# A LayerNorm input of a local-attention network: one half of its shifted copy moved from ScalarE to VectorE

## What is computed

```
def shift_tokens(t):
    a, s = jnp.split(t, 2, -1)
    s = jnp.pad(s, ((0, 0), (1, 0), (0, 0)))[:, :-1]
    return jnp.concatenate([a, s], -1)

def ffn_layer(x, g, bln, W1, b1, W2, b2):
    mu = x.mean(-1, keepdims=True)
    var = ((x - mu) ** 2).mean(-1, keepdims=True)
    xn = (x - mu) / jnp.sqrt(var + 1e-05) * g + bln
    hg = xn @ W1 + b1
    a, gate = jnp.split(hg, 2, -1)
    return a * jax.nn.gelu(gate, approximate=False) @ W2 + b2

for i in range(DEPTH):
    x = attn_layer(shift_tokens(x), Wqkv[i], q_scale[i], k_scale[i], Wo[i]) + x
    x = ffn_layer(shift_tokens(x), ln_g[i], ln_b[i], W1[i], b1[i], W2[i], b2[i]) + x
```

## Time and profile before

| | us |
|---|---|
| median of 3 runs | 1779.91 |
| lowest and highest run | 1777.05 to 1782.78 |
| the profiled execution | 1762.38 |
| its span | 1760.6 |
| TensorE busy | 1601.1 |
| DVE busy | 1228.2 |
| ACT busy | 1153.2 |
| POOL busy | 1003.2 |

### The profile page before, as it was taken

How to read it: one execution, slowest core, us unless ns; L and a number is a source line. 1 busy time by engine, 2 the same in 40 slices (tenths; PEclk the granted TensorE clock), 3 DMA queues, 4 the chain that set the end, 5 groups by cost and what they waited for, 6 DMA issues and landing times. The chain is left out here.

```text
span 1760.6 us, 75862 instructions
## 1 busy us (share of the span) xinstructions
PE 1601.1 (91%) x33590; PEld 1298.7 (74%) x33590; DVE 1228.2 (70%) x1912; ACT 1153.2 (65%) x2115; POOL 1003.2 (57%) x757
## 2 busy tenths in 40 slices
PE   5879999989999999999999899999999999999976
PEld 4557778777777877877777777777778777777765
DVE  7666677677677667767767776776776777677662
ACT  2246676767767766776776666776676676767644
POOL 2155566666565756646666664675565586566551
PEclk9999999999999999999999999999999999999996
DMA  3266665675765567566567656657755666665650
GB/s 129 57 169 148 154 144 135 152 182 134 165 151 127 137 153 198 132 147 157 122 153 201 144 130 145 154 126 186 169 135 138 153 146 143 150 157 123 151 125 25
DMA packets 98568, 252.97 MB, mean 144 GB/s; under 512 B 30016, under 2 KB 36288, under 8 KB 97472
## 3 DMA queue, kind: packets, MB, share of 16 engines
q1 hardware_dynamic: 98240, 248.12, 59.0%
HBM read 44.59 MB, written 2.10 MB: 27 GB/s over the span
## 5 line engine op out<-in xcount | busy, mean ns | idle before, releaser
L805 DVE SCALAR_TENSOR_TENSOR UV<-ps,veca,rope 128x512 f32<-128x512 f32 x768 | 531.2, 744 | 184.5 <-PE ps L381 155.3
L1212 POOL TENSOR_TENSOR KK<-UV 128x512 f32<-128x512 f32 x192 | 241.9, 1282 | 406.6 <-DVE UV L805 403.4
L957 ACT ACTIVATE sq<-ps 128x512 f32<-128x512 f32 (+1 forms) x400 | 228.1, 583 | 263.0 <-PE ps L381 172.4
L1212 POOL TENSOR_TENSOR Qtb<-UV 128x512 f32<-128x512 f32 x192 | 242.9, 1287 | 86.5 <-DVE UV L805 86.5
L381 PE MATMUL ps<-xh,wh 128*128 128x256 f32 x768 | 245.1, 319 | 1.7 <-ACT sq L957 0.8
L1231 POOL TENSOR_TENSOR E<-E,ri 128x1024 f32<-128x1024 f32 x96 | 182.8, 1904 | 79.3 <-DVE ri L878 73.6
L381 PEld LDWEIGHTS ps<-PT,V 64*64 64x64 f32 x12288 | 194.1, 136 | 40.0 <-issue 35.4
L381 PE MATMUL ps<-xh,wl 128*128 128x256 f32 x768 | 218.0, 284 | 3.8 <-issue 3.8
L381 PE MATMUL ps<-xl,wh 128*128 128x256 f32 x768 | 217.7, 283 | 1.0 <-issue 1.0
L381 PE MATMUL ps<-PT,V 64*64 64x32 f32 x12288 | 210.3, 221 | 3.6 <-ACT PT L957 2.0
L1222 POOL TENSOR_TENSOR E<-E,mx 128x1024 f32<-128x1024 f32 x96 | 182.9, 1905 | 51.3 <-DVE mx L872 51.2
(11 more groups left out here) (128 smaller groups left out, 3106.0 us busy)
## 6 DMA issues: line engine op xcount, KB each, us to landing
V<-Vs SPq DMA_DIRECT2D x672, 128.0 KB
KK<-KK SPq DMA_DIRECT2D x384, 128.0 KB
Qtb<-Qtb SPq DMA_DIRECT2D x384, 128.0 KB, 2.4
rope<-in_c_rope SPq DMA_DIRECT2D x48, 512.0 KB, 4.1
raw<-in_Wqkv SPq DMA_DIRECT2D x6, 1536.0 KB, 7.9
V<-Vs SPq DMA_DIRECT2D x96, 64.0 KB
V<-V SPq DMA_DIRECT2D x96, 64.0 KB, 2.0
wo<-in_Wo SPq DMA_DIRECT2D x6, 512.0 KB, 6.5
```

Of the source, the lines that this page charges most:

```text
L805: e.scalar_tensor_tensor(UV[:, p % 2, slot, :].rearrange("p (i t) -> p i t", i=2), ps[:, half, :].rearrange("p (i t) -> p i t", i=2), veca ...
L957: return e.activation(out, in_, f, **kw)
L1212: e.tensor_tensor(dst, u, v, op).then_inc(s["rot_done"], 1)
```

## The change

On DVE a new entry `c_xz` stands right behind `c_xb`. It waits until DVE's own residual has been written and until `zl` of the step before has been computed, and copies rows 0 to 63 of the residual to `zs`. ACT's `c_xs` keeps the copy of rows 64 to 127. It waits for DVE's copy, by the new semaphore `zx_done`, in place of `zl_done`. `z_act` is then raised once a step, and `c_mu` waits for that. The list gains one entry; its line breaks are new, the order of the others isn't.

```diff
-    b_sub0 b_s0 a_rot1 b_nrm0 a_sqx0 a_mx1 b_s1 a_my1 a_x1 a_y1 c_xb a_sqy1 a_rl c_wo w_h0 b_s2 b_sum0 b_sub1
+    b_sub0 b_s0 a_rot1 b_nrm0 a_sqx0 a_mx1 b_s1 a_my1 a_x1 a_y1 c_xb c_xz a_sqy1 a_rl c_wo w_h0 b_s2 b_sum0 b_sub1
...
             def c_mu(j, _):
-                e.wait_ge(s["z_act"], j * 2 + 2)
+                e.wait_ge(s["z_act"], j + 1)
                 mm(ps[:, WO, 0:T], cen[:, :], zs[:, :]).then_inc(s["mu_done"], 1)
...
+            def c_xz(j, _):
+                x0 = j % 2 * T
+                e.wait_ge(s["xb_done"], j * C + C)
+                if j:
+                    e.wait_ge(s["zl_done"], j)
+                e.tensor_copy(zs[0:hf, :], XB[0:hf, x0 + 1:x0 + 1 + T]).then_inc(s["zx_done"], 1)
...
                 e.wait_ge(s["xb_done"], j * C + C)
                 e.wait_ge(s["cb_done"], j // 2 + 1)
-                if j:
-                    e.wait_ge(s["zl_done"], j)
-                act(zs[0:hf, :], XB[0:hf, x0 + 1:x0 + 1 + T]).then_inc(s["z_act"], 1)
+                e.wait_ge(s["zx_done"], j + 1)
                 act(zs[hf:, :], XB[hf:, x0:x0 + T]).then_inc(s["z_act"], 1)
```

More of the change, by code:

```diff
@@ L57 @@
 SCHEDULE = """b_rcq a_mx0 a_xs+1 a_vs0 a_v0 a_v1 b_rq a_my0 a_x0 a_xh+1 b_scale0 a_rot0 a_vs1 a_y0 b_lnq b_max0 a_sqy0 b_rqt
-    b_sub0 b_s0 a_rot1 b_nrm0 a_sqx0 a_mx1 b_s1 a_my1 a_x1 a_y1 c_xb a_sqy1 a_rl c_wo w_h0 b_s2 b_sum0 b_sub1
+    b_sub0 b_s0 a_rot1 b_nrm0 a_sqx0 a_mx1 b_s1 a_my1 a_x1 a_y1 c_xb c_xz a_sqy1 a_rl c_wo w_h0 b_s2 b_sum0 b_sub1
     a_norm0 a_xl+1 w_h1 a_sqx1 b_exp0 c_xs c_zl a_rck c_mu w_l0 b_s3 c_var b_nrm1 c_zsq a_halo a_x2 a_lnk a_rot2
[L60 to L63, removed]
+    c_rs a_rot3 a_y2 a_rh a_sqy2 b_pt0 b_pto0 b_scale1 b_pt1 c_zh b_att0 w_l2 b_max1 b_att1 a_sp0 b_pto1 a_sqx2 c_h0
+    c_zn b_exp1 a_mx2 a_sp1 a_my2 b_oto0 c_gelu0 b_sum1 b_wo a_x3 c_wl c_gelu1 a_kn0 b_pto2 c_h1 b_pt2 c_hm0 a_y3
+    a_kn1 a_mx3 a_sqy3 a_sqx3 b_pt3 c_hm1 c_wh b_att2 c_h2 a_norm1 w_h2 a_my3 c_hm2 b_att3 b_pto3 c_down c_gelu2
+    c_fin b_xb w_l1 b_oto1""".split()
 LAG = {"w": 0, "a": 0, "b": 1, "c": 2}
@@ L237, in program @@
             rh_done rl_done rkb_done khat_done k_halo rqt_done rq_done s_done e_done m_done sub_done p_done rs_done
-            ri_done pt_done pts_done pn_done o_done ots_done wo_done xb_done cb_done z_act mu_done
+            ri_done pt_done pts_done pn_done o_done ots_done wo_done xb_done cb_done z_act zx_done mu_done
             zsq_done var_done zln_done rstd_done zn_done zb_done zh_done zl_done h_done gelu_done hm_done w2_done
@@ L950, in _ @@
             run({"a_mx": a_mx, "a_my": a_my, "a_rck": a_rck, "b_rcq": b_rcq, "a_kn": a_kn, "b_rq": b_rq, "b_scale": b_scale,
-                 "b_max": b_max, "b_sum": b_sum, "b_xb": b_xb, "c_xb": c_xb, "c_zn": c_zn,
+                 "b_max": b_max, "b_sum": b_sum, "b_xb": b_xb, "c_xb": c_xb, "c_xz": c_xz, "c_zn": c_zn,
                  "c_hm": c_hm, "c_fin": c_fin}, tail)
```

## The result

| | before | after |
|---|---|---|
| median, us | 1771.55 | 1777.76 |
| lowest and highest | 1754.40 to 1782.78 | 1771.05 to 1788.24 |
| runs | 20 | 20 |
| the profiled execution | 1762.38 | 1772.32 |
| its span | 1760.6 | 1770.5 |

The ratio is 1.0045, with a 95% interval of 1.0025 to 1.0065: +8.0 us (4.4 to 11.5). The runs of before have a lower median here than the three shown ahead of the prediction (1779.91), so the absolute times of the prediction lie some 8 us high; what it says of the change is not touched by that.

The account below looks back on a forecast made before the run. TensorE, busy 91% of the span, bounds the kernel, its wait for zs lying on the path. 37 steps x 0.11 us = +4.1 us, the other 11 nothing; 1779.91 + 4.1 = 1784.0 us, range 1769 to 1790.

Parts of the forecast that it names:

- TensorE's hole for zs sets the step: At the product of zs with cen, TensorE waits 28.2 us in 37 steps; any loss or gain there passes on whole.
- nothing behind zs runs by a clock of its own: Later TensorE holes (PT, the queries' DMA) end with work TensorE itself released, so they move along with zs.
- The copy alone, 0.28 us: DVE's 64x256 copy to zs takes 0.28 us without POOL, reckoned from SBUF-to-SBUF copies of 512 and one column.
- The copy is held by POOL: DVE's copy behind XB waits for POOL's running rotation half to end at 867.41, and itself ends at 867.56.
- ScalarE's half starts at 867.59: ACT's copy starts 0.03 us behind DVE's, ends at 868.00; the matmul starts at 868.05, 0.11 us later than before.
- the likeliest one (0.50): DVE's copy is held until POOL's instruction ends: +0.11 us in each of 37 steps, +4.1 us; chance 0.50.
- a copy that isn't held (-9.2 us): Rival: DVE's copy to zs runs freely beside POOL; each of 37 steps gains 0.25 us, 1770.7 us; chance 0.18.
- one at a single rate (-4): Rival: DVE's copy moves one column at a time, unheld, 0.42 us; -0.11 us a step, 1776 us; chance 0.05.
- The slow release (+8.9 us): Rival: DVE's held copy ends 0.28 us behind POOL's end, not 0.15; +0.24 us a step, 1788.8 us; chance 0.17.
- POOL's second half in front (+49 us): Rival: POOL's second rotation half goes before DVE's copy, which waits to 868.63; +1.33 us a step, 1829 us; chance 0.05.
- Removed ACT copies bring nothing further, `rs` is 0.31 us late and covered at the transposes: Dropping 48 ScalarE copies (20 us busy) gains nothing more; DVE's sum over E, 0.31 us late, delays no transposes.
- the two covers (0.56 and 0.50 us): Slack behind DVE's copy: 0.56 us before TensorE wants POOL's normalised E, 0.50 us before DVE's E<-ps; both absorb 0.31 us.

Follow-up runs that it names:

- side by side: Changed kernel, but ScalarE's half no longer waits for DVE's copy and the product with cen waits for both halves; 0.9965 of the kernel before, median 1764.32 us.
- the second experiment: Changed kernel, but ACT's copy waits for zx_done first and no longer for xb_done; 1.0016 of the kernel before, +2.8 us (-0.7 to +6.5).

## Why the prediction was right, and where it was off

- **TensorE's hole for zs sets the step**: right for losses. By their middle values one more copy on ACT and the change itself passed on 80% or more of what the offset says. The gains passed on less, for reasons that are in part open. The statement that nothing behind zs runs by a clock of its own was wrong for gains: the clamp and POOL's E don't wait for zs.
- **The copy alone, 0.28 us**: 285 ns at the least. Right.
- **The copy is held by POOL**: right. 618 ns in the middle, end 0.15 us behind that of POOL's instruction, 0.65 behind XB's, where 0.15 and 0.66 were forecast. The count ahead of it was slightly off: in before a half of the key rotation runs at XB's end in 45 steps, not 44, mostly with 0.51 us left, not 0.48. The rule of the Trainium skill ("SBUF — State Buffer", section "Who interferes with whom") agrees with these rows, and with the reduction too, which isn't such a copy and never exceeded 414 ns. It would not by itself have given the sign: side by side, with the held copy, the kernel is faster.
- **The step that was mis-sized: "ScalarE's half starts at 867.59"**, 0.03 us behind the copy. Measured: 0.11 us. I had taken the gap from other pairs of releaser and follower. In the order listings ahead of the prediction, ACT's copy already has three waits, `zx_done,cb_done,xb_done`; in before the late one was the one carried by the instruction, and after the change the late one is `zx_done`, an instruction of its own. So the term was +0.20 us a step and not +0.11, and the sum 37 x 0.20 = +7.4 us and not +4.1. Measured: +8.0 (4.4 to 11.5), while TensorE's wait for zs grew by 5.7 in the profiles. With the hand-off as I had reckoned it (the second experiment) the offset was the forecast's 1.15 and the time +2.8.
- **So the case was the likeliest one (0.50), but its total fell beyond the bound of 0.3%**, on the side that I had given 0.38 and not the 0.42 of no change. The predicted 1784.0 lies 6.2 us above the measured 1777.76: 8.4 of it come from the level of the first three runs (1779.91 against 1771.55), less 2.1, by which the two medians differ more (6.2) than the forecast 4.1. That the two errors go against each other is luck, and the 1784.0 looks better for it than the sum behind it was: the change costs about twice the forecast 4.1. The range, 1769 to 1790, holds the measured median.
- **Rivals**: a copy that isn't held (-9.2 us) and one at a single rate (-4) fell with the 618 ns. The slow release (+8.9 us) came out near the measured time, but by another mechanism: the copy's end is 0.15 behind POOL's and not 0.28, and the rest is the hand-off. POOL's second half in front (+49 us) fell for one copy; the doubled copy shows what it costs when it happens.
- **Removed ACT copies bring nothing further, `rs` is 0.31 us late and covered at the transposes**: right. `rs` starts 0.59 us behind XB's end (0.28 before), and the wait of the transposes for PT is unchanged. The change leaves no new wait for POOL's E in TensorE's list. What the two covers (0.56 and 0.50 us) missed is a third one on the same path, clamp to ACT's `R`, 0.45 us. The change shows no loss there, because zs is late too; in the experiments that gain it is used up.
- **Wait for zs near 32 us**: 33.9.

## What to carry to other kernels

When a piece of work is split over two engines to shorten it, let the consumer wait for both halves; a half that waited for the other gave back here all that the split gained, and more, because the DVE copy took its 0.28 us only when POOL was idle. Where an instruction has several waits, look in the trace which of them ends last and whether the instruction carries it. Here the late one was carried when it stood first and the wait that it implied was dropped. And before you count on a gain, list every cover on the path behind, since what doesn't hang on the gain can be next to set the step, and look at what the edit adds to the queue of the engine that is the bottleneck.

## What was not expected of the hardware

- A wait that stands as an instruction of its own costs 0.08 us when it is the last to end: 0.11 us from DVE's end to ACT's start, against 0.03 when ACT's copy carries it. The wait for `cb_done`, long met, costs nothing that shows: it stands there too, and the gap is 0.03.
- A held copy gets in before the POOL instruction that is next and shows as started (POOL at 874.34, the copy ends at 874.53), but a second copy right behind does not: in 44 of 48 steps it waited for that one's end (1.35 us in the middle of them).
- A fp32 move as a reduction over an axis of length one takes 411 ns for 256 columns against 285 for the copy, and wasn't held by POOL in any of 48 cases. Beside POOL it is the faster of the two (the copy's median is 618).
- Two DVE operations of 128 and 127 columns to different halves of the partitions started 0.31 us apart, each taking 0.27 to 0.29 us, so nothing of them overlapped; XB and the copy behind it, in the change, start 0.32 us apart too, and there a wait stands between them.
- In the kernel with the doubled copy TensorE's granted clock averaged 0.96 from 250 to 1500 us, in before 1.00. TensorE had more idle time in that kernel; the runs don't show more of the cause than that.
- TensorE's larger holes without a releaser recur at the same products in kernels whose TensorE queue has the same instructions, and lie at others when it has one wait more a step: 1.9 to 2.5 us at one place in eight kernels, 2.7 to 4.1 us at another in four.
